# Left and right values change places in the directed layers' order of projecting, splitting and combining

## The reference

```
u = h @ h.T / sqrt(384);  p = softmax(u);  delta = p * adj
attn = delta / (sum(delta, -1) + 1e-10)
h_left, h_self, h_right = h @ W_left.T + b_left, h @ W_self.T + b_self, h @ W_right.T + b_right
ctx = where(j > i, attn, 0) @ h_left + diag(attn) * h_self + where(j < i, attn, 0) @ h_right
o = relu((ctx - mean) / sqrt(var + 1e-12) * gamma + beta)
```

## Time and profile before

| | |
|---|---|
| median of 3 runs | 2752.53 us (2752.3 to 2755.15) |
| profiled execution | 2754.08 us, its span 2752.5 us |
| busy share of the span | PE 92%, PEld 68%, DVE 85%, ACT 66%, POOL 53% |
| L1, 661 to 1110 us | PE 431.98, DVE 417.02, ACT 254.86, POOL 329.89 of 449.00 us; granted clock 1.00 |
| L2, 1150 to 2025 us | PE 849.90, DVE 744.77, ACT 490.30, POOL 626.24 of 875.00 us; granted clock 0.99 |

### The profile page before, as it was taken

The page is one execution under the profiler, slowest core; times in us unless marked ns, Lnnn a source line. Parts: engine busy times, 40 slices in busy tenths (PEclk is TensorE's granted clock), DMA queues, the critical chain, the costliest instruction groups (busy, mean ns, idle before and its releaser), DMA issues. The chain is left out here.

```text
span 2752.5 us, 86859 instructions
## 1 busy us (share of the span) xinstructions
PE 2520.6 (92%) x27969; PEld 1884.4 (68%) x27969; DVE 2336.4 (85%) x9515; ACT 1804.1 (66%) x4409; POOL 1453.0 (53%) x2016
## 2 busy tenths in 40 slices
PE   5999999986999999699999999999969999999998
PEld 4888888874666665466666666666648888888886
DVE  5778777776999999688888888888859999999997
ACT  5888888874555555455555555555538777777775
POOL 1233232324777777477777777777734434444443
PEclk9999999997999999799999999999979999999998
DMA  3011010102000000100000000000000000000000
GB/s 105 28 30 29 28 30 27 30 14 88 9 9 10 10 10 9 46 10 10 10 10 10 10 10 10 10 10 10 10 6 22 24 25 23 27 23 27 23 27 23
DMA packets 73988, 60.19 MB, mean 22 GB/s; under 512 B 7888, under 2 KB 73936, under 8 KB 73936
## 3 DMA queue, kind: packets, MB, share of 16 engines
q1 hardware_dynamic: 73936, 59.54, 7.1%
HBM read 46.92 MB, written 12.58 MB: 22 GB/s over the span
## 5 line engine op out<-in xcount | busy, mean ns | idle before, releaser
L149 PE MATMUL bank<-L_w_hi,L_hT_hi 128*128 128x384 f16 x2112 | 691.7, 327 | 0.0
L151 PE MATMUL bank<-L_w_hi,L_hT_lo 128*128 128x384 f16 x2112 | 691.5, 327 | 0.0
L150 PE MATMUL bank<-L_w_lo,L_hT_hi 128*128 128x384 f16 x2112 | 691.4, 327 | 0.0
L550 ACT ACTIVATE raw_weights<-L_minus_scores,L_minus_max 128x128 f32<-128x128 f32 x1536 | 476.0, 389 | 69.5 <-DVE L_minus_max L665 67.7
L149 PE MATMUL bank<-L_hT_hi,L_w_hi 128*128 128x128 f16 x2304 | 413.4, 220 | 1.7 <-issue 1.2
L150 PE MATMUL bank<-L_hT_lo,L_w_hi 128*128 128x128 f16 x2304 | 413.3, 220 | 0.0
L151 PE MATMUL bank<-L_hT_hi,L_w_lo 128*128 128x128 f16 x2304 | 413.2, 220 | 0.0
L665 DVE CUSTOM_DVE_ANT_0 L_minus_scores<-bank,L_minus_score_bias 128x128 f32<-128x128 f32 x1536 | 347.8, 282 | 11.4 <-PE bank L834 5.9
L692 DVE TENSOR_TENSOR L_pT_lo<-bank,L_pT_hi 128x512 f16<-128x512 f32 x384 | 241.0, 682 | 126.6 <-ACT L_pT_hi L572 126.5
L1069 ACT ACTIVATE L_e<-bank,L_nmax 128x128 f32<-128x128 f32 x192 | 70.6, 368 | 365.6 <-DVE L_nmax L1154 365.6
L151 PEld LDWEIGHTS bank<-L_w_hi,L_hT_lo 128*128 128x128 f16 x2112 | 207.5, 98 | 138.2 <-issue 2.5
(11 more groups left out here) (165 smaller groups left out, 7531.3 us busy)
## 6 DMA issues: line engine op xcount, KB each, us to landing
adj_tile<-in_adj SPq DMA_DIRECT2D x320, 64.0 KB, 1.8
x<-in_x SPq DMA_DIRECT2D x64, 192.0 KB, 2.3
out<-L_result SPq DMA_DIRECT2D x64, 192.0 KB, 1.9
raw_weights<-in_L_gnn_Wq SPq DMA_DIRECT2D x2, 576.0 KB, 4.0
raw_weights<-in_L_gnn_Wk SPq DMA_DIRECT2D x2, 576.0 KB, 5.7
raw_weights<-in_L_gnn_Wv SPq DMA_DIRECT2D x2, 576.0 KB, 5.5
raw_weights<-in_L_gnn_Wl SPq DMA_DIRECT2D x2, 576.0 KB, 4.9
raw_weights<-in_L_gnn_Ws SPq DMA_DIRECT2D x2, 576.0 KB, 4.8
```

Of the source, the lines that this page charges most:

```text
L149: pe.matmul(out, stat[0], move[0], start=first, stop=False)
L150: pe.matmul(out, stat[0], move[1], start=False, stop=False)
L151: return pe.matmul(out, stat[1], move[0], start=False, stop=last)
L550: last = act.activation(probs[:, n_.slot(k), i, :], scores[:, i, :], ACT.Exp, bias=nmax[:, n_.slot(k), i:i + 1], scale=-1.0)
```

## The change

In every `step` of the directed layers right takes left's place and left takes right's. TensorE projects the right values first and the left ones second; the transpose of the masked exponentials stays inside the second projection. The combining starts with three matmuls of the right values and ends with those of the left. ScalarE makes `right_hi` ahead of `sides_hi` and `left_hi` behind the normed context. GpSimd still makes `right_lo`, now ahead of `sides_lo`. VectorE still makes `left_lo`, which moves from behind the second `biased` to behind `stats` and `mean_var`, directly ahead of `turned_lo`.

```diff
 # GpSimd
                             if n_.has(0):
+                                right_lo(n_)
                                 sides_lo(n_)
-                                right_lo(n_)
...
 # ScalarE
-                                values_hi(n_, d["l_sum"], d["l_hi"], left, leftv[0])
+                                values_hi(n_, d["r_sum"], d["r_hi"], right, rightv[0])
                                 sides_hi(n_)
                             if n_.has(-1):
                                 norm_ctx(n_, -1)
                             if n_.has(0):
-                                values_hi(n_, d["r_sum"], d["r_hi"], right, rightv[0])
+                                values_hi(n_, d["l_sum"], d["l_hi"], left, leftv[0])
...
 # VectorE
                                 diagonal(n_)
-                                biased(n_, d["l_psum"], d["l_sum"], d["l_lo"], left, l_bank, tables[n_.kind()][2])
+                                biased(n_, d["r_psum"], d["r_sum"], d["r_lo"], right, r_bank, tables[n_.kind()][3])
...
                                 scaled_denominator(n_)
-                                biased(n_, d["r_psum"], d["r_sum"], d["r_lo"], right, r_bank, tables[n_.kind()][3])
-                                left_lo(n_)
+                                biased(n_, d["l_psum"], d["l_sum"], d["l_lo"], left, l_bank, tables[n_.kind()][2])
                                 scaled_eps(n_)
                             if n_.has(-2) and n_.kind(-2) != "first":
                                 add_to_x(n_, -2)
                             if stats_ahead:
                                 stats(n_, 2)
                                 mean_var(n_, 2)
+                            if n_.has(0):
+                                left_lo(n_)
                             if n_.has(1):
                                 turned_lo(n_, 1)
...
 # TensorE
-                                if part == 2 and c == 0:
+                                if part == 0 and c == 0:
...
+                                project(n_, 2, r_bank, d["r_psum"])
                                 project(n_, 0, l_bank, d["l_psum"])
-                                project(n_, 2, r_bank, d["r_psum"])
...
                                 wait(pe, d["a_lo"], n_.done())
+                                wait(pe, d["r_lo"], n_.done())
+                                three_products(pe, c_bank[:, 0:D], (sidesv[0][:, 1, :], sidesv[1][:, 1, :]),
+                                               (rightv[0][:, :], rightv[1][:, :]), first=True, last=False)
+
+                                wait(pe, d["l_hi"], n_.done())
+                                pe.matmul(c_bank[:, 0:D], sidesv[0][:, 0, :], leftv[0][:, :], start=False, stop=False)
+                                pe.matmul(c_bank[:, 0:D], sidesv[1][:, 0, :], leftv[0][:, :], start=False, stop=False)
                                 wait(pe, d["l_lo"], n_.done())
...
+                                pe.matmul(c_bank[:, 0:D], sidesv[0][:, 0, :], leftv[1][:, :], start=False, stop=True)\
                                     .then_inc(d["c_psum"], 1)
```

More of the change, by code:

```diff
@@ L1329, in step @@
                                 wait(pe, d["a_lo"], n_.done())
-                                wait(pe, d["l_lo"], n_.done())
[L1331 to L1338, removed]
+                                wait(pe, d["r_lo"], n_.done())
[4 more added lines that the diff above has]
+                                pe.matmul(c_bank[:, 0:D], sidesv[1][:, 0, :], leftv[0][:, :], start=False, stop=False)
+                                wait(pe, d["l_lo"], n_.done())
+                                pe.matmul(c_bank[:, 0:D], sidesv[0][:, 0, :], leftv[1][:, :], start=False, stop=True)\
                                     .then_inc(d["c_psum"], 1)
```

## The result

The changed kernel takes 2860.77 us (median of 4 runs, 2859.9 to 2861.66) against 2752.44 (4 runs): 1.0391 times as long, 95% interval 1.0373 to 1.0409. The forecast was 2872. The profiled execution took 2861.66, its span is 2860.1.

The account below looks back on a forecast made before the run. TensorE's stream plus gaps was taken to bound the directed layers; L1's 58.6 and L2's 61.1 add 119.7 to the profiled 2754.08, giving 2873.8, or 2872 after the 1.6 offset to the median; range 2775 to 2895.

Parts of the forecast that it names:

- The turn's bound: In both directed layers a turn costs what TensorE streams plus its gaps; L1 averages 6.955 before the change.
- "second" turn: L2 turn with `add_to_x` and no `stats`; 7.07 before, forecast 7.02, as waiting `left_lo` is served ahead of `gain`.
- `left_lo` behind `gain`: In L1 and L2's "first" turns `left_lo` waits for `gain`, ending 0.42 behind it; turns cost 0.945 and 1.02 more.
- the earlier trace: L3 row: a 128x12 VectorE operation starting inside GpSimd's 1.81 us f32 addition takes 1.43; taken as sign that `gain` blocks.
- Rival 1: VectorE wins the race against `gain` in L2's "first" turns, a pair costing 0.21: 2824 in all; chance 0.13.
- Rival 2: `gain` does not block `left_lo`; L1 costs 16.4 us, L2 13 us: 2782 in all; chance 0.10.
- Rival 3: The port doesn't bind in the new order; `scaled_eps` and `add_to_x` pass beside `right_lo`: faster, 2712; chance 0.07.
- "first" turns: L2 turns with `stats` and no `add_to_x`; 6.56 before, forecast cost 1.02, with `gain` ahead of `left_lo` by 0.12.
- Rival 4: `left_lo` loses to `gain` in L2's "second" turns too, about +1.0 x 63: 2935; chance 0.04.
- The late `sides_lo`: On GpSimd behind `right_lo` and `add_to_x`, `sides_lo` ends at +6.00 in L1, so the combining starts at +6.05, 0.55 later.
- The loop's gap: TensorE's extra 0.30 at L2's loop turn back goes, the stall lying six matmuls ahead; if it stays, 16 us.
- The sum: L1's 58.6 plus L2's 61.1 make 119.7 us on the profiled execution's 2754.08.

Follow-up runs that it names:

- e1: Changed kernel, but `left_lo` subtracts from the PSUM bank of the left projection (one SBUF input, bias missing in the low part): 2774.91 us.
- e3: Changed kernel, but `gain` multiplies only 192 of 384 columns, the other half staying zero: 2815.57 us.
- e5: Changed kernel, but `left_lo` stands behind `turned_lo` and `var_eps` on VectorE: 2886.08 us.
- e7: Kernel before, but in L2's "second" turns, except at the phase's edges, `add_to_x` stands behind `turned_lo`: 2731.31 us.
- e2: Changed kernel, but GpSimd makes `sides_lo` ahead of `right_lo` again: 2786.22 us.
- e6: Kernel before, but `add_to_x` moves from behind `scaled_eps` to behind the context's statistics: 2769.18 us.

## Why the prediction was right

- *The turn's bound.* TensorE's stream plus gaps, in both kernels. The "second" turn, where the combining's six matmuls end a turn without a wait, is 6.96 against 7.02 forecast.
- *`left_lo` behind `gain`.* Forecast by bounds, since no row of before had the pair; the earlier trace rows, which tipped it, has one SBUF input and 12 columns, so it is another form of operation and did not show this pair. e1 and e3 show it from two sides: take the second SBUF input away, and 86 us go; shorten `gain` by 0.41, and the turns that wait for it shorten by 0.41 and 0.40. Rivals 1, 2 and 3 fall with the rows above: the lead of 0.12 in "first" turns was 0.10 and held.
- *Rival 4* did not come in this kernel (1304.00 against 1304.56), but e5 shows that it is real.
- *The late `sides_lo`.* The combining starts at +6.07 in L1 (816.27), forecast +6.05. It decides the "second" turns; what is left over in e1 it shares with `hT_lo`, which ends the turn there by 0.1. The forecast's 7.90 has the same order: `hT_lo` last, the combining inside it.
- *The loop's gap.* The "second" turn's 0.30 went, as I took it. In e7, where the last matmul waits for nothing, 0.37 lie between its start and the next similarity across the jump; in the "second" turns of the changed kernel and of e2, where TensorE was held up six matmuls ahead, 0.16. So it goes when the wait is that far ahead; that TensorE's queue fills meanwhile is argued, not shown.
- *The sum.* L1: turns of 7.87 and 7.81, 7.84 on average (forecast 7.90), 0.885 x 62 = 54.9 where I had 58.6. L2: 14.54 against 13.63 a pair, 0.91 x 63 = 57.3 where I had 61.1. That makes 112.2, but the profiled executions differ by 107.6, 12.1 less than the forecast sum of 119.7. From the first to the last similarity of a phase L1 grew by 54.2 and L2 by 54.3, so 3.0 of the missing 4.6 are edge turns of L2 that grew by less than a steady pair; the rest lies in L1's edges and outside both phases. What made both terms too large by 4 us each: in L1 `right_lo` starts at +4.04 or, in the turn from 818.07, +3.96, not at +4.06, and in the "second" turn from 1298.71 at +3.96, not at +4.04, since `hT_lo` now sets the start of the turn and VectorE goes straight on to the context.

The rule of the Trainium skill, page "SBUF — State Buffer", section "Who interferes with whom", that a Vector instruction with two SBUF inputs and a GpSimd one that reads SBUF exclude each other for the whole of the first to start, agrees with the traces: 1.23 and 1.32 for `left_lo` behind `gain`, 0.525 with one input in PSUM. It does not hold for every pair: in the kernel before, the masking (L1160, a fused multiply and sum with both inputs in SBUF) starts in 117 turns while GpSimd's one-column power (L995, 0.55) is running, and takes its usual 0.29. Whether that form is exempt or the power had read its input by then, no run shows.

## What to carry to other kernels

Where two engines exclude each other, price a moved operation by what the other engine runs at that moment: here 0.55 us of work became 1.32 because it came 0.10 us too late. Something short ahead of a critical step should be in line before the other engine's long operation comes up, or take one input from PSUM, where the value is there to take. An uncritical operation (`add_to_x`) belongs behind the last critical one of both engines; ahead of the chain that starts the turn it put the masking off by 0.55, its whole length, and made the turns 0.12 to 0.17 longer (e6).

## What was not expected of the hardware

- The first matmul of the combining starts 0.15 behind the end of the GpSimd operation it waits for (1345.50 to 1345.65) and 0.09 behind `sides_lo` in the changed kernel (816.18 to 816.27), where the last one starts 0.05 behind.
- GpSimd's multiplication (`gain`) of 192 columns takes 0.59, of 384 columns 1.00: by these two, an estimated 0.18 do not shrink with the size.
